# A convolution, a router and two products in one kernel: arguments, sines and decays earlier in the iteration, and a kernel's row from one matmul

## What is computed

```python
# 1. a state-space convolution per channel h
dt = exp(log_dt); A = -exp(log_A_real) + 1j * A_imag
Cs = (C[..., 0] + 1j * C[..., 1]) * (exp(A * dt) - 1) / A
K  = 2 * einsum('hn,hnl->hl', Cs, exp(A * dt * arange(1024))).real    # 64 complex states
u  = x * (arange(1024) < length[:, None])
y  = (causal convolution of u with K + u * D) * the same mask
# 2. a router over 64 experts of rank 16, 16 taken, on each row of y
scores = y @ Wr.T; gates = softmax over the 16 largest, 0 elsewhere
h   = einsum('nd,krd->nkr', y, A_ffn)
out = x + 2 * einsum('nkr,kdr->nd', h * gates[:, :, None], B_ffn)
```

## Time and profile before

| | |
|---|---|
| median of 3 runs | 907.69 us (907.43 to 908.87) |
| profiled execution | 908.42 us |
| its span | 906.6 us |
| mean granted clock of TensorE over the span | 0.996 of full speed |
| busy share | TensorE 98%, its weight loads 87%, VectorE 81%, ScalarE 42% |
| DMA | 99.85 MB in 67123 packets, 110 GB/s |

### The profile page before, as it was taken

One profiled execution on the slowest core, in us unless ns is written; L12 is line 12 of the kernel. 1 busy time (PEld: TensorE's weight loads), 2 busy tenths in 40 slices (PEclk: granted clock), 3 DMA queues, 4 the chain that ended last, 5 costly groups with the idle time before them and its releaser, 6 DMA issues.

```text
span 906.6 us, 15546 instructions
## 1 busy us (share of the span) xinstructions
PE 888.0 (98%) x4536; PEld 791.1 (87%) x4536; DVE 738.0 (81%) x2473; ACT 380.9 (42%) x655; POOL 2.0 (0%) x12
## 2 busy tenths in 40 slices
PE   5999998999999999999999999999999999999998
PEld 3667997988899988899998899998889998889997
DVE  8899987788898888898888888888889888888722
ACT  4762544444434444534344433354443444442100
POOL 0000000000000000000000000000000000000000
PEclk9999998999999999999999999999999999999999
DMA  6621324443334444334444333444333444433331
GB/s 221 249 57 47 76 54 110 111 131 102 104 107 110 110 133 108 102 112 100 110 133 114 105 117 104 106 119 131 101 105 108 110 110 133 108 101 114 85 98 47
DMA packets 67123, 99.85 MB, mean 110 GB/s; under 512 B 22944, under 2 KB 49184, under 8 KB 67104
## 3 DMA queue, kind: packets, MB, share of 16 engines
q1 hardware_dynamic: 66400, 99.16, 40.0%
q10 hardware_dynamic: 704, 0.46, 0.2%
HBM read 60.52 MB, written 34.87 MB: 105 GB/s over the span
## 4 chain that ended last, share of the span: by engine, by line
PE 90%; DVE 6%; DMA 1%; ACT 1%; issue 1%; ACTq 0%; SPq 0%; DVEq 0%
PE out_ps L1241 25%; PE h_ps L1241 17%; PE out_ps L1245 12%; PE h_ps L1245 9%; PE turn_ps L1241 7%; PE turn_ps L1245 4%; PE conv_ps L1197 2%; PE conv_ps L1198 2%; PE conv_ps L1199 2%; PE conv_ps L1207 1%; PE conv_ps L1180 1%; PE conv_ps L1208 1%; PE conv_ps L1209 1%; PE conv_ps L1181 1%; PE conv_ps L1182 1%; PE h_ps L1250 1%
## 5 line engine op out<-in xcount | busy, mean ns | idle before, releaser
L1241 PE MATMUL out_ps<-b_lo,g_hi 128*128 128x512 f32 x496 | 195.5, 394 | 0.0
L1241 PE MATMUL out_ps<-b_hi,g_hi 128*128 128x512 f32 x496 | 195.4, 394 | 0.0
L1241 PE MATMUL h_ps<-a_hi,y_hi 128*128 128x384 f32 x480 | 161.4, 336 | 0.0
L1241 PE MATMUL h_ps<-a_lo,y_hi 128*128 128x384 f32 x480 | 161.2, 336 | 0.0
L1245 PE MATMUL out_ps<-b_hi,g_lo 128*128 128x512 f32 x496 | 122.9, 390 | 0.0
L1245 PEld LDWEIGHTS out_ps<-b_hi,g_lo 128*128 128x128 f32 x496 | 93.1, 188 | 20.3
L1241 PEld LDWEIGHTS out_ps<-b_lo,g_hi 128*128 128x128 f32 x496 | 93.3, 188 | 19.6
L1241 PEld LDWEIGHTS out_ps<-b_hi,g_hi 128*128 128x128 f32 x496 | 93.5, 188 | 18.8
L717 DVE SCALAR_TENSOR_TENSOR z<-swapped,step_other,part 128x64 f32<-128x64 f32 x384 | 92.3, 281 | 12.0
L710 DVE SCALAR_TENSOR_TENSOR part<-z,step_own,conv_ps 128x64 f32<-128x64 f32 x384 | 90.4, 277 | 8.5
L1245 PE MATMUL h_ps<-a_hi,y_lo 128*128 128x384 f32 x480 | 93.0, 336 | 0.0
(11 more groups left out here) (216 smaller groups left out, 1496.7 us busy)
## 6 DMA issues: line engine op xcount, KB each, us to landing
xt_in<-in_xt SPq DMA_DIRECT2D x32, 512.0 KB, 3.3
x_in<-in_x SPq DMA_DIRECT2D x62, 256.0 KB, 3.7
out<-x_in SPq DMA_DIRECT2D x62, 256.0 KB, 3.1
moved<-square_sb SPq DMA_DIRECT2D x28, 512.0 KB, 2.6
square_sb<-moved SPq DMA_DIRECT2D x112, 128.0 KB, 2.9
b_in<-in_b_t SPq DMA_DIRECT2D x8, 512.0 KB, 6.0
a_in<-in_a_t SPq DMA_DIRECT2D x8, 512.0 KB, 7.1
t_lo<-k_sb SPq DMA_DIRECT2D x62, 64.0 KB, 4.2
```

Source lines behind the costliest of these rows:

```text
L1241: pe.matmul(o, hi[:, c, :], moving[:, c, columns], start=first and c == order[0] and moving is w_hi, stop=False)
```

## The change

Four things change together.

1. From tile 5 on (`ROWED = LAGGED + 2`, the sixth tile) the kernel's row comes from one matmul instead of two. ScalarE writes `row_in` as `out_raw` times `real_only` (1 on real partitions, 0 on imaginary ones) in fp32r, behind `o_hi`. VectorE's `low_row` shuffles `o_lo` by 16 partitions (SWAP), so that the low parts of the real partitions come to lie on the imaginary ones, multiplies by `imaginary` (1 on imaginary partitions) and adds `row_in`. High parts then stand on the real partitions and low parts on the imaginary ones, and one matmul with a matrix of ones sums over all. For that `real` is rewritten to ones once, at tile 5. The shuffled low parts are put into `turned`, so `arguments` now waits for `s_row`.
2. On VectorE `arguments(t + 3)` moves from behind `low_moved_in` (in `step(3)` `low_in`) to right behind `low_row`, and `add_skip(t + 2)` from ahead of `make_powers` to behind `turn_powers`.
3. On ScalarE `sines(t + 3)` and `decays(t + 3)` move ahead of `copy_k(t + 2)`; `theta(t + 4)` stays behind it.
4. On SyncE `send_powers` moves ahead of `load_near`, and `bring_powers` ahead of `store_rows`.

```diff
             def high_out(t):
@@
                 act.activation(o_hi[:, :, :], out_raw[:, :, :], ACT.Copy).then_inc(s_ohi, 1)
+                if isinstance(t, int) and t < ROWED:
+                    return
+                if not (isinstance(t, int) and t == ROWED):
+                    act.wait_ge(s_kps, t)
+                act.activation(row_in[:, :, :], out_raw[:, :, 0:P], ACT.Copy, scale=real_only[:, :]).then_inc(s_rhi, 1)
@@ scalar, step
+                if table:
+                    sines(t + 3)
+                    decays(t + 3)
+                if prep:
                     copy_k(t + 2)
-                if table:
-                    tables(t + 3, more=not last_table)
+                if table and not last_table:
+                    theta(t + 4)
@@ vector
             def arguments(t):
+                if not (isinstance(t, int) and t <= ROWED):
+                    dve.wait_ge(s_row, t - ROWED)
@@
+            def low_row(t):
+                if isinstance(t, int) and t == ROWED:
+                    dve.wait_ge(s_kps, ROWED)
+                    dve.tensor_scalar(real[:, :], phase_own[:, :].to_broadcast([P, P]), 0.0, 1.0, ALU.mult, ALU.add).then_inc(s_ones, 1)
+                dve.wait_ge(s_olo, t + 1 - EXACT)
+                dve.sem_inc(s_passed, 1)
+                dve.stream_shuffle(low_swapped, o_lo[:, :, 0:P].bitcast(F32), SWAP).then_inc(s_rswap, 1)
+                dve.wait_ge(s_rhi, t + 1 - ROWED)
+                dve.wait_ge(s_rswap, t + 1 - ROWED)
+                dve.scalar_tensor_tensor(out=row_in[:, :, :], in0=low_swapped, scalar=imaginary[:, :],
+                                         in1=row_in[:, :, :].bitcast(F32), op0=ALU.mult, op1=ALU.add).then_inc(s_row, 1)
+            low_swapped = turned[:, :, 0, 0:P]
@@ vector, start
+            dve.tensor_scalar(real_only[:, :], phase_own[:, :], 4.0, None, ALU.mult)
+            dve.tensor_copy(imaginary[:, :], odd[:, :])
@@ vector, step
                     low_out(t + 2)
+                    low_row(t + 2)
+                if table:
+                    arguments(t + 3)
...
-                if table:
-                    arguments(t + 3)
                 if not second:
                     add_rows(t - 1, 0)
-                if prep:
-                    add_skip(t + 2)
                 if table:
                     make_powers(t + 3)
                     turn_powers(t + 3)
+                if prep:
+                    add_skip(t + 2)
                 add_rows(t - 1, 1)
@@ tensor
             def kernel_row(t):
-                pe.wait_ge(s_olo, t + 1 - EXACT)
-                pe.matmul(k_ps, real[:, :], o_hi[:, :, 0:P], start=True, stop=False)
-                pe.matmul(k_ps, real[:, :], o_lo[:, :, 0:P], start=False, stop=True).then_inc(s_kps, 1)
+                if isinstance(t, int) and t < ROWED:
+                    pe.wait_ge(s_olo, t + 1 - EXACT)
+                    pe.matmul(k_ps, real[:, :], o_hi[:, :, 0:P], start=True, stop=False)
+                    pe.matmul(k_ps, real[:, :], o_lo[:, :, 0:P], start=False, stop=True).then_inc(s_kps, 1)
+                    return
+                if isinstance(t, int) and t == ROWED:
+                    pe.wait_ge(s_ones, 1)
+                pe.wait_ge(s_row, t + 1 - ROWED)
+                pe.matmul(k_ps, real[:, :], row_in[:, :, :], start=True, stop=True).then_inc(s_kps, 1)
@@ sync, step
+                if table:
+                    send_powers(t + 3)
                 if prep:
                     load_near(t + 2)
                 if table:
-                    send_powers(t + 3)
+                    bring_powers(t + 3)
                 store_rows(t - 1)
-                if table:
-                    bring_powers(t + 3)
```

More of the change, by code:

```diff
@@ L156, in build @@
         square_in = sb("square_in", [P, HT * P])
+        row_in = sb("row_in", [P, HT, P], F32R)
+        imaginary = sb("imaginary", [P, 1])
+        real_only = sb("real_only", [P, 1])
         conv_ps = [ps(f"conv_ps{i}", [P, NC * B]) for i in range(HT)]
@@ L193, in build @@
             sem(n) for n in ("s_theta", "s_whole", "s_args", "s_sine", "s_decay", "s_powers", "s_other", "s_raw"))
-        s_ohi, s_olo, s_turned, s_inhi, s_inlo, s_kps, s_kcopy, s_kdone = (
-            sem(n) for n in ("s_ohi", "s_olo", "s_turned", "s_inhi", "s_inlo", "s_kps", "s_kcopy", "s_kdone"))
+        s_rhi, s_rswap, s_row, s_ones, s_ohi, s_olo, s_turned, s_inhi, s_inlo, s_kps, s_kcopy, s_kdone = (
+            sem(n) for n in ("s_rhi", "s_rswap", "s_row", "s_ones", "s_ohi", "s_olo", "s_turned", "s_inhi", "s_inlo", "s_kps", "s_kcopy", "s_kdone"))
         s_thi, s_tlo, s_xhi, s_xlo, s_near = (sem(n) for n in ("s_thi", "s_tlo", "s_xhi", "s_xlo", "s_near"))
@@ L231, in build @@
         TURNED = LAGGED + 3
+        ROWED = LAGGED + 2
         block = ctx.enter_context(nc.Block())
@@ L493, in high_squares, with tables @@
                                square_sb[:, :].rearrange("p (q c x) -> p c q x", q=JM, c=NE), ACT.Copy).then_inc(s_ghi, 2)
-            def tables(t, more=True):
+            def tables(t):
                 sines(t)
                 decays(t)
-                if more:
-                    theta(t + 1)
+                theta(t + 1)
             def first_step():
```

## The result

| | before | after |
|---|---|---|
| median, 6 runs each | 907.73 us (907.43 to 908.87) | 900.72 us (900.6 to 902.25) |
| ratio, 95% interval | | 0.9925 (0.9915 to 0.9935) |
| profiled execution | 908.42 us | 900.60 us |
| its span | 906.6 us | 898.8 us |
| mean granted clock over it | 0.996 | 1.000 |

The kernel is 7.0 us faster. 900.1 us was predicted, with 898.9 to 904.0 as the range.

A forecast was written before the change was run, and what follows sets the result against it. TensorE's matmuls were taken to bound the kernel from 160 us on, with one large hole before. Gains of 3.1 and 4.5 us, 7.6 in all, took the profiled 908.42 to 900.8, the median to 900.1 us; range 898.9 to 904.0.

The forecast's parts named there:

- The steady part: Tiles 6 to 31: one matmul of 256 columns fewer each, 26 x 0.12 = 3.1 us if nobody makes TensorE wait.
- The row's margin: In the loop, the row would be ready some 2 us before TensorE asks for it.
- the idle time takes the 1.1 us: In the loop, VectorE's idle 2.22 us before the powers would absorb the row, so states and t_lo start as before.
- the ring: Found afterwards: VectorE's arguments, ScalarE's sine, table load and decays, VectorE's powers, then VectorE's work to the next arguments.
- The rival on the slower side: In the loop, a row costing over 3.5 us delays TensorE every iteration; 919 us at a row of 4.0; chance 0.05.
- t_lo's 1.3: In the loop, t_lo's margin of 1.3 us before TensorE wants it, counted as room for the row.
- The hole at tile 3: TensorE's wait for t_lo and half clock vanish, a new 2.3 us wait precedes tile 5's feed; gain 4.5 us.
- The clock: the rival: The new 2.3 us hole before tile 5's feed drops TensorE's clock, giving 902.9 us; chance 0.21.
- My price of 2.8 us: Cost of a clock fall in the new hole at tile 3, taken from the old place: 5.16 - 2.61 + 0.25.
- the 0.73 us between before's profile and its median: Whole kernel: the median lay 0.73 us below the profiled 908.42 us, so 900.8 became 900.1 us.

The follow-up runs named there:

- e2: The changed kernel with all moves but without the row's work, the kernel's row from two matmuls everywhere: 903.60 us.
- e1: The changed kernel with the row in one matmul but all moves undone, at tile 3 too: 929.76 us.
- e3: The changed kernel with the moves only in tile 3's step, the loop in the old order with the row in one matmul: 927.06 us.
- e6: The changed kernel with the arguments back behind in_lo in the loop only, sines and decays still ahead of the row's copy: 929.22 us.
- e8: The changed kernel with the row's shuffle and scalar_tensor_tensor done twice on VectorE in the loop: 907.39 us.
- e7: The changed kernel with sines and decays behind the row's copy again in the loop only, arguments still early: 900.96 us.
- e11: The changed kernel run again unedited, on the same chip as the runs with tile 3's sines late or 1.2 us more there: 900.96 us.
- e9: The changed kernel with y's low parts written twice on VectorE in tile 3's step, 1.2 us more ahead of in_lo: 903.79 us.

## Why the prediction was right, and where it wasn't

The two parts came out as forecast, 4.7 us at tile 3 (4.5 predicted) and 3.1 us behind it (3.1 predicted). The first was understood. The second was right by luck in one step.

**The steady part: the size right, one reason wrong.** The matmul gives 0.12 us an iteration (0.12 predicted), with e2 as the control. The row's margin is 1.8 us (2 predicted), in_lo's 405.09 - 402.83 = 2.3 us (2.7). The row costs VectorE 1.46 us (422.84 to 424.64, less the 0.34 that o_lo takes), where I had 1.1 within 0.65 to 1.5: the hand-overs inside VectorE take 0.27, 0.11 and 0.15 us where I had two of 0.1; I forgot that the arguments wait for the row as well.

The step that failed is "the idle time takes the 1.1 us", with "with sines and decays ahead of the copy" as its reason. The 2.22 us before the powers were no slack; they were part of the ring. With them in place e1 and e3 have iterations of 27.86 us, 1.07 more than after and 0.94 more than before, for a row of 1.23 us, and e6 27.95. It is the arguments' move that opened the ring, by laying the transpose and three splits, which VectorE had to do anyway, over ScalarE's part of it. I had booked that move only as a cost to in_lo. The sum came out right since both moves were made, which is luck as far as this step goes; a reader who kept my reason would have dropped the arguments' move as harmless and lost 28 us.

What room before had can be bounded now. 27.86 less the row's 1.23 us in e3 (406.34 to 407.91, less 0.34) is 26.63 us for VectorE's ring, against 26.92 of TensorE: 0.3 us. This is an estimate. In ScalarE's timeline of before
```profile
405.60 0.39 ACT L423 ACTIVATE k_sb<-h_ps 128x256 f32<-128x256 f32 x1 [1.86 <-PE h_ps L1168]
406.00 1.28 ACT L387 ACT_TABLE_LOAD   x1
407.30 0.64 ACT L387 ACTIVATE turned<-args 128x520 f32<-128x520 f32 x1
```
it is to be seen as the copy's wait for TensorE, which starts the table load so late that the sine comes at 407.30, 0.27 us after the arguments were done (their second instruction was begun at 406.33 and took 0.70).

**The rival on the slower side had the wrong threshold.** I let it decide at a row of 3.5 us, the 2.22 us and t_lo's 1.3 added to what was taken. By e8 0.78 us are free behind the row as it is, and it is 1.46 us, so this rival decides near 2.2 us, and the first to be late is the row's own matmul, not t_lo. My 0.05 was too small for that: the upper end of the row's range, 1.5 us, lay 0.7 us from the edge and not 2.0.

**The hole at tile 3: right in every step.** In us, predicted and measured: feed 137.2 and 137.03; decays end 136.55 and 136.72; powers 137.05 and 136.89; t_lo ends 149.44 and 149.26; near product 150.24 and 150.36; down product 152.85 and 152.97. The rewrite to ones took 0.22 us, not the 0.80 of the start. The wait is given as 1.8 us, 2.3 predicted: the feed is 137.03 - 135.00 = 2.0 us later than before, and the view counts from the modelled end of the matmul ahead.

**The clock: the rival was a matter of executions.** In the profiled one the clock stayed at 1.000; in 5 of 16 executions of after and e7 it did not. I had given 0.21. My price of 2.8 us was too high: the executions with the lower mean clock are some 1.5 us longer. e6's trace shows why, with the same step: the clock is low for the feed and a part of the product behind it, 1.6 us in all, and not for the convolution. No trace was taken of such an execution of after itself. The Trainium skill ("TensorE: Matmul & The Clock Gate", Part 1) has the check run free of the kernel, so that the same gap may or may not be caught. These executions agree: the same kernel in the same job gives both (e11: 0.998 once, 0.999 and more four times).

**The 0.6 us by which the median missed** come from the step from profile to median. Profile to profile the change gave 7.8 us for 7.6 predicted. But I took the 0.73 us between before's profile and its median over to after. In the last job before's executions at a mean clock of 0.997 or 0.998 took 907.46 to 907.91 us, two at 0.996 took 908.37 and 908.78: the profiled one, 908.42 at 0.996, was of those. Its trace has a low clock only from 150 to 158 us, so its 0.7 us most likely lay in the clock of the hole that the change removes; no trace of a shorter execution is there to compare. After's profiled execution lies 0.12 us below its median.

**SyncE's order and the skip** cost nothing to be seen, as predicted. t_lo's loads are issued at 405.19 where the feed begins at 405.09, 3.2 us later against it than before (2.7 predicted), and no wait on them appears in the loop. Neither was undone alone in the changed kernel.

Open: how often the clock falls at 2 us of hole. It did in 5 of 16 executions of after and e7, and in 12 of 21 of the versions that have the same hole and short waits in the loop besides.

## What to carry to other kernels

Before work is booked into an engine's idle time, follow the releaser back: if it was itself started by an earlier instruction of the same engine, the idle time is a piece of a ring and holds nothing; only a wait that ends on the engine that sets the pace is room, and here 0.78 us were free where that wait was 0.67. To shorten such a ring, move its first instruction ahead of work that must be done anyway. A margin towards the pacing engine is used once, idle time in a loop each time. And read the mean clock of every execution before a hole's price, or the offset between profile and median, is taken from one.

## What the runs showed of the hardware

- The clock fell 0.6 us and more after TensorE had resumed from a hole of 3.3 us (e9, 138.39 us; 0.61 in 139 to 140 us), and was at 1.00 again in 143 to 144 us, with TensorE busy throughout. Behind a hole of 2.0 us (e6, feed at 136.99 us) it was 0.78 in 137 to 138 us, 0.50 in the next two and at 1.00 again in 141 to 142 us; in after's profiled execution, with the same step, it stayed at 1.00.
- A matmul of 256 columns whose weight load had waited and began 0.03 us ahead of it fills 0.36 us (e8), and 0.11 us where the load stands 0.22 us ahead, beside the matmuls before it (after).
- STREAM_SHUFFLE of 128x256 f32 takes 0.45 us; SCALAR_TENSOR_TENSOR of 128x256 with fp32r out 0.48 us; TENSOR_SCALAR 128x128 to fp32r from one broadcast column 0.22 us at 130 us, where the same took 0.80 us at 2.2 us.
